# Main attention: the six prepared blocks of the next pair of heads placed at other score tiles

## The chip, the cores and the metric

The kernel runs on one core of one Trainium2 chip. The metric is the device time of one execution in microseconds (us). A core has TensorE (PE in the profile), VectorE (DVE), ScalarE (ACT), GpSimd (POOL) and SyncE (SP, which here issues the transfers). Each runs its own list of instructions in order, and they wait for each other on semaphores.

## The reference

Two transformer blocks on x of 1024 tokens by 256. The change lies in the first block's main attention, 16 heads over all 1024 tokens:

```
q_mid = rmsnorm(h @ q_a_w.T);  q = q_mid @ q_b_w.T          # per head: 128 nope + 64 rope
kv_lora, k_pe = split(h @ kv_a_w.T)                         # 64 latent, 16 heads x 64 rope
q_pe, k_pe = apply_rope(q_pe), apply_rope(k_pe)             # x * cos + rotate_half(x) * sin
scores = (q_nope.k_nope + q_pe.k_pe) * 192 ** -0.5
probs  = softmax(scores);  ctx = probs @ v;  main_out = ctx @ o_w.T
```

The key's nope part and the values come from the 64 latents, so the kernel folds those weights into the query: a head's score is a product over 64 rope rows and 64 latent rows. The rest (a 16-head pattern attention ahead of it, an 8-expert layer behind it, then the second block with a causal attention and 16 experts) is not touched.

## The kernel before

**Tiles and units.** The main attention works on pairs of heads p = 0 to 7. A pair has four units u = 4p to 4p + 3 (256 queries each), and a unit four score tiles (128 queries by 1024 keys of one head). `main_order` writes one list, and each engine takes from it the steps that are its own, in that order. A unit on PE is: six matmuls of score tile 0 (L1834 to L1836, `pe_score`), the output product of two units ago (L1972), tile 1, tile 2, half of the last unit's probabilities times values (128 small matmuls, L1938), tile 3, the other half. Scores are held in two slots of PSUM. DVE takes the maximum of a tile (L1843) and turns the exponentials (L1871), ACT takes the exponentials (L1858).

**Prepared blocks.** Before a pair's scores can start, its queries and keys have to be made from the latents, in six blocks of 128 x 512, in the order `FIRST = (R0, R1, R2, Q0, R3, Q1)`: R0 and R1 the rope keys (two halves of the tokens), R2 and R3 the rope queries, Q0 and Q1 the latent queries. A block k of pair p takes these steps:

- PE: five or six matmuls of 128 x 512 (`pe_prep`, L1569), after the copy of the block two before it.
- ACT: a copy out of PSUM into a staging tile t (`act_product`, L1623). There are two staging tiles, taken in turn, so a copy first waits until POOL and the transfers have let go of the block two before.
- SP, for rope blocks only: four transfers that swap rows inside t (`sp_swap`, L1637).
- POOL: for a rope block times cosine (L1650), then, with the swap landed, times sine (L1652), the sum (L1655), two roundings (L1669) and two remainders (L1676); for a latent block only the roundings and remainders. Behind Q0 it splits the next key weights, and behind Q1 the next latent and rope query weights (L1736 to L1758).

The first score tile of a pair waits for R0, R1, R2 and Q0 on POOL, the one of its third unit (4p + 2) for R3 and Q1. POOL's list has the blocks one behind the other and is not written by `main_order`.

**Places.** A block stands at a number of a score tile, counted from the first tile of the pair before it: number 4 is tile 0 of the second unit, 16 is tile 0 of the pair itself. Only numbers that leave 0 or 1 over when divided by 4 (tiles 0 and 1 of a unit) are asked for in `main_order`. On PE the block follows the output product or tile 1, on ACT it follows the exponentials of tile 0 (at tile 0) or stands ahead of those of tile 1 (at tile 1).

**SP's list.** Per unit SP has four transfers of the row sums (`sp_shares`, L1906) that wait for DVE's reciprocal (L1891 to L1898), two that spread them (`sp_spread`, L1919), and behind these the unit's swaps. At unit 28 it also issues the expert weights (L2302) once the last swap is out.

Of the kernel before, what the change touches and what calls it, by code (L numbers as in the profile page):

```python
# [71 lines left out]
    (31, 1): [("normed", 0)],  # L72
}

PREP_AT = (5, 8, 9, 12, 16, 17)


def main_order():

    order = [("expo", 0, 1), ("score", 0, 2), ("ctx", 0), ("ctx", 1), ("vturn", 0, 0), ("expo", 0, 2), ("score", 0, 3),  # L80
             ("cadd", 0), ("ctx", 2), ("vturn", 0, 1), ("cadd", 1), ("expo", 0, 3), ("ctx", 3), ("cadd", 2), ("vturn", 0, 2),
             ("cadd", 3)]
    preps = {16 * (p - 1) + at: (p, i) for p in range(1, 8) for i, at in enumerate(PREP_AT)}

    def prep(n, kind):
        if n in preps:
            order.append((kind, *preps[n]))

    def output(u):
        if u >= 0:  # L90
            order.extend([("project", u), ("add", u)])

    for u in range(1, 32):
        order.append(("score", u, 0))
        output(u - 2)
        prep(4 * u, "prep")
        order.extend([("rec", u - 1), ("spread", u - 1), ("vturn", u - 1, 3), ("expo", u, 0)])
        prep(4 * u, "pcopy")
        order.extend(BESIDE_LAST.get((u, 0), ()))
        order.append(("score", u, 1))  # L100
        prep(4 * u + 1, "prep")
        prep(4 * u + 1, "pcopy")
        order.extend([("vturn", u, 0), ("expo", u, 1)])
        order.extend(BESIDE_LAST.get((u, 1), ()))
        order.extend([("score", u, 2), ("pv", u - 1, 0), ("vturn", u, 1), ("expo", u, 2)])
        order.extend([("score", u, 3), ("pv", u - 1, 1), ("lift", u - 1), ("vturn", u, 2), ("ot", u - 1), ("expo", u, 3)])
    output(30)
    order.extend([("rec", 31), ("spread", 31), ("vturn", 31, 3), ("turn", 0), ("pv", 31, 0), ("pv", 31, 1), ("hT", 0),
                  ("wup", 1), ("wdown", 1), ("lift", 31), ("ot", 31), ("project", 31), ("logits", 0), ("add", 31)])
    return order  # L110
# [197 lines left out]
def program(nc, a, out):  # L308
# [841 lines left out]
    def act_fold(e, step):  # L1150
# [6 lines left out]
        else:  # L1157
            rows, dst, h0, _ = fold_rows(g - 4)
            e.activation(dst[0:rows, h0:h0 + 8, :].rearrange("p h c -> p (h c)"), bank[fold_bank(g)][0:rows, :],
                         ACT.Copy).then_inc(fold_ok, 1)  # L1160

    PATTERN, MAIN, CAUSAL = pattern_order(), main_order() + experts_order(), causal_order()

    g0, a0_ok, hf_ok, bias_ok, add_ok = (sem(n) for n in ("g0", "a0_ok", "hf_ok", "bias_ok", "add_ok"))
# [2131 lines left out]
```

## Time and profile before

| | |
|---|---|
| median of three runs | 1306.22 us (1299.85 to 1313.52) |
| the profiled execution | 1304.03 us, span 1302.2 us |
| busy in the span | PE 1189.6 us (91%), DVE 891.5 (68%), ACT 654.2 (50%), POOL 532.7 (41%) |
| main attention, from its first tile in this list to its last product | about 270 to 778 us of the span |
| chain that ended last | PE 61%, DVE 12%, POOL 12% |

A line of a timeline gives start, duration, engine, line and operation, and in brackets how long the engine had been idle before and for whom it waited. The matmuls overlap, so the distance from start to start tells more than a duration. The "granted clock" is 1.0 at TensorE's 2.4 GHz and 0.5 at 1.2 GHz.

### The profile page before, as it was taken

How to read it: one execution, taken by the hardware profiler on the slowest of the kernel's cores; microseconds unless marked ns; L12 is line 12 of the kernel's file. 1: busy time of each engine (PE TensorE's matmuls, PEld its weight loads, DVE VectorE, ACT ScalarE, POOL GpSimd, SP SyncE). 2: the span in 40 equal slices, each digit the busy share in tenths (PEclk: the TensorE clock that was granted, in tenths of full speed). 3: DMA queues.
4: the chain of work that ended last, by engine and by line, in shares of the span. 5: the costliest groups of instructions: out<-in, count | busy, mean ns of one | idle time of the engine just before them, and what ended most of it. 6: DMA issues, size and time to landing. Idle time of an engine off the chain costs nothing.

```text
span 1302.2 us, 34623 instructions
## 1 busy us (share of the span) xinstructions
PE 1189.6 (91%) x14433; PEld 836.3 (64%) x14436; DVE 891.5 (68%) x1354; ACT 654.2 (50%) x1242; POOL 532.7 (41%) x531
## 2 busy tenths in 40 slices
PE   8999999997979898979797869999998998989997
PEld 5544334466767676767675657888853444678997
DVE  4689988367868687868675875645668673755555
ACT  3479978853434343434342424333245676435553
POOL 4257264327576666657575323544200000421221
PEclk8989999999989898989898978999999999989999
DMA  7780000011111111101010122010332410101110
GB/s 276 206 178 2 2 17 25 1 45 32 31 30 32 31 40 27 45 25 44 23 35 21 58 63 85 25 52 23 85 73 64 94 37 1 34 17 33 50 41 33
DMA packets 41699, 66.25 MB, mean 51 GB/s; under 512 B 8476, under 2 KB 27676, under 8 KB 40604
## 3 DMA queue, kind: packets, MB, share of 16 engines
q1 hardware_dynamic: 41544, 64.04, 17.8%
q8 instruction: 115, 1.88, 0.6%
q14 instruction: 40, 0.33, 0.1%
HBM read 45.60 MB, written 8.45 MB: 42 GB/s over the span
## 4 chain that ended last, share of the span: by engine, by line
PE 61%; DVE 12%; POOL 12%; issue 4%; ACT 4%; SPq 3%; DMA 3%; POOLq 0%; ACTq 0%; DVEq 0%
PE bank L1478 8%; PE bank L2148 6%; PE bank L2149 6%; PE bank L2150 6%; PE bank L1435 4%; PE bank L1938 4%; POOL qk0l L1676 3%; PE bank L1834 3%; PE bank L1298 3%; PE bank L1569 2%; PE bank L1972 2%; PE bank L1836 2%; PE bank L1835 2%; PE bank L1415 2%; DVE mpc L1377 2%
## 5 line engine op out<-in xcount | busy, mean ns | idle before, releaser
L1843 DVE TENSOR_REDUCE nmq<-bank 128x1 f32<-128x1024 f32 x128 | 155.1, 1212 | 95.8 <-PE bank L1836 94.3
L1858 ACT ACTIVATE P<-bank,nmq 128x1024 f32<-128x1024 f32 x128 | 142.8, 1115 | 144.6 <-DVE nmq L1843 143.8
L1456 ACT ACTIVATE Pb<-bank 128x512 f32<-128x512 f32 (+3 forms) x355 | 180.7, 573 | 31.6 <-PE bank L1435 10.9
L1306 DVE TENSOR_REDUCE mp<-bank 128x2 f32<-128x1024 f32 x128 | 153.5, 1222 | 29.7 <-PE bank L1298 28.9
L1834 PE MATMUL bank<-qk1h,qk0h 128*128 128x512 f32 x256 | 113.3, 443 | 46.7 <-POOL qk0l L1676 39.8
L1871 DVE STREAM_TRANSPOSE PT<-P 128x1024 f32<-128x1024 f32 x124 | 151.8, 1224 | 0.9 <-ACT P L1858 0.9
L1938 PE MATMUL bank<-PT,kv 32*64 32x128 f32 x7936 | 137.0, 275 | 7.9 <-issue 7.8
L1938 PEld LDWEIGHTS bank<-PT,kv 32*64 32x64 f32 x7936 | 118.5, 130 | 34.0 <-issue 33.8
L1377 DVE TENSOR_REDUCE mpc<-bank 128x2 f32<-128x1024 f32 (+2 forms) x96 | 88.3, 953 | 44.4 <-PE bank L1365 22.0
L1478 PE MATMUL bank<-Pb,vx 128*17 128x256 f32 (+3 forms) x1222 | 107.1, 411 | 0.7 <-ACT OTa L1492 0.5
L1836 PE MATMUL bank<-qk1h,qk0l 128*128 128x512 f32 x256 | 104.4, 408 | 0.7 <-issue 0.7
L1835 PE MATMUL bank<-qk1l,qk0h 128*128 128x512 f32 x256 | 104.1, 406 | 0.7 <-issue 0.7
L1834 PEld LDWEIGHTS bank<-qk1h,qk0h 128*128 128x128 f32 x256 | 49.7, 194 | 66.8 <-issue 50.2
L1652 POOL TENSOR_TENSOR t<-t,sinT 128x512 f32<-128x512 f32 x32 | 41.0, 1281 | 99.7 <-DMA t<-t 99.7
L2123 POOL TENSOR_TENSOR cTt<-cTt,gab 128x256 f32<-128x256 f32 x8 | 6.1, 760 | 179.9 <-DVE cTt L2118 179.7
L2349 POOL TENSOR_TENSOR hl<-hf,hh 128x512 fp32r<-128x512 f32 x32 | 41.7, 1305 | 90.4 <-ACT hh L2336 90.4
L1949 ACT ACTIVATE other<-bank 64x256 f32<-64x256 f32 x64 | 24.3, 379 | 97.1 <-PE bank L1938 96.3
L1435 PE MATMUL bank<-qstr,kstr 64*128 64x512 f32 x256 | 71.5, 499 | 0.6 <-ACT Pb L1456 0.6
L2563 POOL TENSOR_TENSOR v1l<-wr,v1h 128x512 fp32r<-128x512 f32 x25 | 32.1, 1287 | 95.0 <-ACT v1h L2558 95.0
L1650 POOL TENSOR_TENSOR Rt<-t,cosT 128x512 f32<-128x512 f32 x32 | 41.1, 1284 | 68.6 <-ACT t L1623 65.7
L1435 PEld LDWEIGHTS bank<-qstr,kstr 64*128 64x128 f32 x256 | 28.3, 185 | 58.0 <-ACT Pb L1456 36.6
L1415 PE MATMUL bank<-qst,kst 107*128 107x512 bf16 (+3 forms) x192 | 53.9, 330 | 7.8 <-ACT qst L1402 3.5
(354 smaller groups left out, 2912.9 us busy)
## 6 DMA issues: line engine op xcount, KB each, us to landing
t<-t SPq DMA_DIRECT2D x128, 64.0 KB, 2.4
wr<-wf SPq DMA_DIRECT2D x25, 256.0 KB, 2.7
wraw<-wf SPq DMA_DIRECT2D x8, 768.0 KB, 4.4
scratch<-stgr SPq DMA_DIRECT2D x4, 1024.0 KB, 4.0
Rs<-shares SPq DMA_DIRECT2D x64, 64.0 KB, 2.8
scratch<-stg SPq DMA_DIRECT2D x8, 384.0 KB, 2.6
qst<-scratch SPq DMA_DIRECT2D x9, 256.0 KB, 7.6
owT<-owT SPq DMA_DIRECT2D x1, 2048.0 KB, 11.5
```

What stands on the lines that cost most here:

```text
L1306: e.tensor_reduce(mp[:, w % 3, :, j, kh], wide[slot][:], AX, ALU.max).then_inc(ring_ok, 1)
L1377: e.tensor_reduce(mpc[:, w // 2 % 3, a0:a0 + 2, j, kh], wide[slot][:, :, 0:c], AX, ALU.max).then_inc(ring_ok, 1)
L1435: e.matmul(bank[b][:], kst2[r, hp, kt * 128:kt * 128 + 128], qst2[r, hp, cols(half)], start=True, stop=True).then_inc(st_mm[0], 1)
L1456: e.activation(PBR[l][i % len(PBR[l])][:, 0:c], bank[b][:, 0:c], ACT.Exp, scale=0.25).then_inc(exp_ok[0], 1)
L1478: last = e.matmul(bank[6][32 * a:32 * a + 17, to:to + c], vx[:, t, h * 17:h * 17 + 17], PBR[l][i % len(PBR[l])][:, q0:q0 + c], start=(t == ...
L1834: e.matmul(o, qh[:, qs], kh[:, ks], start=True, stop=False)
L1835: e.matmul(o, qh[:, qs], kl[:, ks], start=False, stop=False)
L1836: last = e.matmul(o, ql[:, qs], kh[:, ks], start=False, stop=True)
L1843: e.tensor_reduce(nmq[:, n % 8:n % 8 + 1], scores(u, i), AX, ALU.max, negate=True).then_inc(mp_ok, 1)
L1858: e.activation(probabilities(u, i)[:], scores(u, i), ACT.Exp, bias=nmq[:, n % 8:n % 8 + 1], accum_out=sums[:, u % 2, i:i + 1]).then_inc(ex ...
L1871: e.transpose(PT[u % 2][:, :, c:c + 32], source).then_inc(pt_ok, 1)
L1938: last = e.matmul(rest[64 * c:64 * c + 64, g, 64 - 64 * c:192 - 64 * c], kv4[b % 4][rows, b // 4, :], transposed(u, b)[rows, :], start=(b ...
```

## The change

The six places of a pair's blocks become one tuple per pair. Pair 1 keeps its first four places and has R3 at 13 and Q1 at 16 (before: 16 and 17). Pairs 2 to 7 have R0 at 1, R1 at 5, R2 at 9, Q0 at 12, R3 at 13 and Q1 at 16 (before: 5, 8, 9, 12, 16, 17). What each block does is the same.

```diff
-PREP_AT = (5, 8, 9, 12, 16, 17)
+PREP_AT = ((5, 8, 9, 12, 13, 16),) + ((1, 5, 9, 12, 13, 16),) * 6
...
-    preps = {16 * (p - 1) + at: (p, i) for p in range(1, 8) for i, at in enumerate(PREP_AT)}
+    preps = {16 * (p - 1) + at: (p, i) for p in range(1, 8) for i, at in enumerate(PREP_AT[p - 1])}
```

In blocks per unit, the four units of a pair (from its own first unit) had 2 (its own R3 and Q1), 1 (next R0), 2 (R1, R2), 1 (Q0). Now they have 2 (own Q1, next R0), 1 (R1), 1 (R2), 2 (Q0, R3).

SP's list from the last unit of pair 0 (u = 3) through the first two of pair 1; L1637 is a swap, L1724 and L1730 are the loads of key and query weights. Before:

```order
L1724 DMA wks<-wkpe 128x256
L1906 DMA shares<-rrow 4x32 x4
L1919 DMA Rs<-shares 64x2x128 x2
L1906 DMA shares<-rrow 4x32 x4
L1919 DMA Rs<-shares 64x2x128 x2
L1637 DMA t_152<-t_152 32x512 x4
L1730 DMA wqs<-wqpe 128x256
L1906 DMA shares<-rrow 4x32 x4
L1919 DMA Rs<-shares 64x2x128 x2
L1637 DMA t_152<-t_152 32x512 x4
```

And now:

```order
L1724 DMA wks<-wkpe 128x256
L1906 DMA shares<-rrow 4x32 x4
L1919 DMA Rs<-shares 64x2x128 x2
L1637 DMA t_152<-t_152 32x512 x4
L1906 DMA shares<-rrow 4x32 x4
L1919 DMA Rs<-shares 64x2x128 x2
L1730 DMA wqs<-wqpe 128x256
L1637 DMA t_152<-t_152 32x512 x4
L1906 DMA shares<-rrow 4x32 x4
L1919 DMA Rs<-shares 64x2x128 x2
L1637 DMA t_153<-t_153 32x512 x4
```

The swap of pair 1's R3 went one unit ahead, and the swap of pair 2's R0 came into the first unit of pair 1, behind the load of the query weights.

ACT's list over the same place, from Q0's copy in u = 3 (L1623 is a block's copy, P the exponentials of a tile). Before:

```order
L1623 ACTIVATE t_153<-bank 128x512
L1858 ACTIVATE P_157,sums<-bank,nmq 128x1024
L1858 ACTIVATE P_158,sums<-bank,nmq 128x1024
L1949 ACTIVATE other<-bank 64x256 x2
L1858 ACTIVATE P_156,sums<-bank,nmq 128x1024
L1858 ACTIVATE P_157,sums<-bank,nmq 128x1024
L1623 ACTIVATE t_152<-bank 128x512
L1623 ACTIVATE t_153<-bank 128x512
L1858 ACTIVATE P_158,sums<-bank,nmq 128x1024
```

And now:

```order
L1623 ACTIVATE t_153<-bank 128x512
L1623 ACTIVATE t_152<-bank 128x512
L1858 ACTIVATE P_157,sums<-bank,nmq 128x1024
L1858 ACTIVATE P_158,sums<-bank,nmq 128x1024
L1949 ACTIVATE other<-bank 64x256 x2
L1858 ACTIVATE P_156,sums<-bank,nmq 128x1024
L1858 ACTIVATE P_157,sums<-bank,nmq 128x1024
L1623 ACTIVATE t_153<-bank 128x512
L1623 ACTIVATE t_152<-bank 128x512
L1858 ACTIVATE P_158,sums<-bank,nmq 128x1024
```

R3's copy moved up behind Q0's, and after the first tile of pair 1 come Q1's copy and then R0's of pair 2. POOL's list is row for row the same; on PE and ACT only the places of the blocks differ.

## Rows read from the trace of the kernel before

**Rows 1.** Waits of 270 to 760 us: total us, times, longest

```profile
POOL t L1652 <- DMA t<-t: 91.9, 20, 8.9
...
PE bank L1834 <- POOL qk0l L1676: 39.8, 7, 6.8
...
PE bank L1938 <- issue: 7.8, 11, 1.5
...
PE bank L1834 <- ACT P L1858: 5.6, 2, 4.0
```

**Rows 2.** Windows: six pairs, first tile of pair 1 to that of pair 7

```profile
core 0: us, PE busy (x) PEld busy (x) DVE busy (x) ACT busy (x) POOL busy (x), PEclk, DMA share, GB/s
...
325.10:698.40 373.30, 326.20 (x7008) 257.01 (x7008) 278.91 (x336) 153.99 (x276) 247.86 (x252) 0.94 0.12 32
```

**Rows 3.** Timeline of PE: start, us, line, count, idle before

```profile
325.11 0.47 PE L1834 MATMUL bank<-qk1h,qk0h 128*128 128x512 f32 x1 [3.85 <-POOL qk0l L1676]
...
431.53 1.13 PE L1972 MATMUL bank<-mo,OTm 128*128 128x256 f32 x4 [0.28 <-DVE OTm L1963]
...
448.26 0.77 PE L1834 MATMUL bank<-qk1h,qk0h 128*128 128x512 f32 x1 [6.07 <-POOL qk0l L1676]
...
450.96 1.53 PE L1972 MATMUL bank<-mo,OTm 128*128 128x256 f32 x4
452.14 0.59 PE L1569 MATMUL bank<-qah,wqh 128*128 128x512 f32 x1
...
463.15 0.50 PE L1834 MATMUL bank<-qk1h,qk0h 128*128 128x512 f32 x1
...
465.08 1.13 PE L1972 MATMUL bank<-mo,OTm 128*128 128x256 f32 x4 [0.28 <-DVE OTm L1963]
465.86 0.58 PE L1834 MATMUL bank<-qk1h,qk0h 128*128 128x512 f32 x1
...
477.95 1.13 PE L1972 MATMUL bank<-mo,OTm 128*128 128x256 f32 x4 [0.29 <-DVE OTm L1963]
```

**Rows 4.** Chain of waits, merged, one block's matmuls at the full clock

```profile
455.05 1.16 PE bank L1569 x5
```

**Rows 5.** Timeline of POOL, first and second unit of pair 3

```profile
462.80 1.28 POOL L1652 TENSOR_TENSOR t<-t,sinT 128x512 f32<-128x512 f32 x1 [7.07 <-DMA t<-t]
...
469.65 1.28 POOL L1669 CAST qk0h<-t 64x512 fp32r<-64x512 f32 x2
471.01 2.64 POOL L1676 TENSOR_TENSOR qk0l<-t,qk0h 64x512 fp32r<-64x512 f32 x2
...
476.27 1.29 POOL L1650 TENSOR_TENSOR Rt<-t,cosT 128x512 f32<-128x512 f32 x1
479.02 1.29 POOL L1652 TENSOR_TENSOR t<-t,sinT 128x512 f32<-128x512 f32 x1 [1.45 <-DMA t<-t]
...
483.17 2.64 POOL L1676 TENSOR_TENSOR qk1l<-Rt,qk1h 64x512 fp32r<-64x512 f32 x2
```

**Rows 6.** Timeline of SP, first unit of pair 3: the swap, the load behind

```profile
458.36 2.92 SPq L1637 DMA_DIRECT2D t<-t  x4
461.32 0.58 SPq L1730 DMA_DIRECT2D wqs<-wqpe  x1
```

**Rows 7.** Timeline of ACT, first unit of pair 3: the second copy

```profile
456.24 0.60 ACT L1623 ACTIVATE t<-bank 128x512 f32<-128x512 f32 x1 [1.94 <-PE bank L1569]
```

**Rows 8.** Groups of DVE's instructions, 270 to 760 us: busy, mean ns

```profile
L1894 DVE TENSOR_TENSOR rsum<-rsum,gat 128x4 f32<-128x4 f32 x31 | 14.0, 453 | 1.1
```

**Rows 9.** Timelines of SP, ACT, POOL and PE around unit 29

```profile
713.25 2.44 SPq L2302 DMA_DIRECT2D wraw<-wf  x2
...
726.58 0.63 ACT L2288 ACTIVATE wh<-wraw 128x512 fp32r<-128x512 f32 x1 [4.97 <-POOL wraw L2282]
...
725.28 1.27 POOL L2282 TENSOR_TENSOR wraw<-wraw,gab 128x512 f32<-128x512 f32 x1
...
728.36 0.73 PE L1834 MATMUL bank<-qk1h,qk0h 128*128 128x512 f32 x1 [3.97 <-ACT P L1858]
```

## The prediction

> **What bounds the kernel now.** I read the page first: PE is busy for 91% of the span, but the mean over the kernel says little of one stage, so I went to the waits of the main attention alone. There PE waits for another engine in one place that counts: the first score tile of a pair waits for the remainder that POOL writes last of Q0, 39.8 us in 7 waits [rows 1]. Its other waits are small: 5.6 us for exponentials, 7.8 us in 11 stops that end without a releaser in the profile (bare stops below). Then the windows of six pairs, from the first tile of pair 1 (325.1) to that of pair 7 (698.4): 373.3 us, in which POOL is busy for 247.9, 66%, and DVE for 278.9, 75% [rows 2]. So POOL is late without being full. What makes it late stands in the same list of waits: 91.9 us in which POOL waits for the swap of a rope block [rows 1].
>
> The timeline of pair 3 shows how. I measure from M, the start of a unit's output product on PE (L1972), since most steps hang on it. In the second unit of this pair M is 465.08 and in the third 477.95, which is 12.87 us for a unit with one block [rows 3]. In the second unit R0 of the next pair is made, and its times sine starts at 479.02, behind a wait for the swap, M + 13.94 [rows 5]. From there POOL needs 485.81 - 479.02 = 6.79 us to the end of the block, and a latent block takes 473.65 - 469.65 = 4.00 us [rows 5]. Before the change R1, R2 and Q0 come in the last two units, so R1's wait for its swap and then three blocks lie in a row ahead of the next pair's first tile. PE is through at 442.19 and starts at 448.26 [rows 3]. DVE and ACT are not in it: they sit idle in that gap too.
>
> **The change, term by term.** It adds and removes no instruction. POOL's list is the same.
>
> 1. Gaps of pairs 2 to 7. 39.8 less the 3.85 of pair 1 [rows 1, 3] is 35.9 us in six gaps. Do they close? The next pair's first tile now needs R2 (made in the third unit at tile 1, alone, just as R0 was in the second unit) and then Q0. With R0's measured distance, R2's sine starts at M2 + 13.94, where M2 is the third unit's product. R2 ends at + 20.73, Q0 about 4.05 later, and PE starts some 0.4 behind it (447.81 to 448.26 [rows 3]; the end is that of the same kind of block [rows 5]): M2 + 25.2. PE itself would be ready at 12.87 for the third unit, plus 10.66 (431.53 to 442.19, a last unit with one block [rows 3]), plus 1.16 for R3's five matmuls [rows 4]: M2 + 24.7. So 0.5 us per gap stays by these rows. If the swap lands 0.5 us sooner nothing stays; if DVE's small product L1894, which stands ahead of the swap's transfers on SP, waits longer, more does. It takes 0.453 us on average [rows 8]. I take 0.5 x 6 = 3.0 us, with 0 at one end and 2 us per gap, 12 us, at the other (four times the row's value). Term: 32.9 us.
>
> The Trainium skill (SBUF — State Buffer, "Who interferes with whom") says that a DVE instruction with two SBUF inputs and a GpSimd one that reads SBUF shut each other out for a whole instruction, and L1894 is such a one. POOL's instructions here take up to 1.29 us, and by that rule L1894 waits more often when POOL is busy for more of the time. Were each L1894 held by one full POOL instruction, 0.8 us more than its mean, the swaps would come that much later and about 5 us would be lost; the row's mean already holds what POOL does to it now, and I go by the row.
>
> 2. The slow clock behind a gap. Behind the 6.07 us of idling the granted clock is 0.5, 1.2 GHz. From the first tile to the product PE takes 450.96 - 448.26 = 2.70 us, against 465.08 - 463.15 = 1.93, and the product 452.14 - 450.96 = 1.18 against 465.86 - 465.08 = 0.78 [rows 3]. That is 1.2 us per gap, in six gaps 7.0 us. A wait of 0.5 us as above should not bring it: the waits of 0.28 us on the product leave the next matmuls fast [rows 3].
>
> 3. Pair 1. Its R0 to Q0 stay, so its first tile stays at 325.11, and the gap of 3.85 us ahead of it [rows 3] stays POOL's. But R3's 1.16 us on PE [rows 4] now lie inside this gap, and the last unit that had two blocks (u = 28) has one. Term: 1.2 us.
>
> 4. Unit 29. There ACT waits 4.97 us for POOL to scale expert weights (L2282 at 725.28, right behind Q1 of pair 7), and PE then waits 3.97 us for exponentials [rows 9]. In the new order R3 of pair 7 is copied a unit ahead, so POOL should be through with Q1 some 13 us after the pair's first tile (worked out in term 5), not 27 (725.28 against 698.4). SP's 3.1 us of the swap are gone ahead of the load of these weights at 713.25 [rows 9], so that load comes sooner too. I take the 3.97 us and 1.2 us of slow clock as in term 2: 5.2 us, between 0 (the load is then what is late) and 5.5.
>
> 5. Other waits, at no cost. R3 and Q1 are needed by the third unit, some 27 us behind the first product. From Q0's end POOL needs 1.2 us for the key weights, 1.4 for a cosine, 6.8 and 4.0: 13.4 us, which is M + 11 in the first unit. The copies on ACT: R0's copy of the next pair stands in the first unit at M + 5.3 (456.24 [rows 7]) and needs the staging tile of R3, whose swap by the same 13.94 lands at M3 + 13.9, which is about the next product (12.87 + 1.16 = 14.0 for a unit with two blocks). That leaves about 5 us. The key weights for R0 are split right behind Q0, 1.2 us, and asked for 5 us later. On SP R0's swap follows the query weights, 0.58 us, and is otherwise where R3's was, M + 7.4 [rows 6]; POOL is then busy with R3 and Q1 to M + 11 and with weights for 2.6 us more (473.65 to 476.27 [rows 5]), so the swap lands beside it. If this cover were gone R0 would come some 3 us later, with R1's swap due only 6 us behind R0's end. So it costs nothing.
>
> Sum: 32.9 + 7.0 + 1.2 + 5.2 = 46.3 us. The profiled execution took 1304.03 us, which gives 1257.7. The median of the runs, 1306.22, lies 2.2 us above it, so I forecast **1260 us** as the median. In its own range of terms (9 us less in term 1, 5 less in term 4; 3 and 0.3 more) it is 1256 to 1274. What is late next is PE itself: with the gaps shut a pair takes (373.3 - 32.9 - 7.0) / 6 = 55.6 us, and DVE's 278.9 / 6 = 46.5 us fit into that.
>
> **Rivals.**
>
> - *Bare stops come to light.* There are 11 stops of at most 1.5 us in 32 units [rows 1], and others may now be hidden in the gaps. One more full stop per pair is 7 x 1.5 = 10.5 us: 1270. For it: PE has never run two pairs without a pause in this stage. Against it: the units between the gaps run on end without one in most places. 0.12.
> - *Half the gap stays.* If R2's swap lands 3 us later than R0's did, because a swap now stands in SP's list in every unit, the gap is 3.5 us, as large as pair 1's, and about the full slow clock with it. Lost against the forecast: 6 x (3.0 + 1.2) = 25 us: 1285. For it: POOL waits 91.9 us for swaps, and the margin in term 1 is nil. Against it: SP's list around R2 in the third unit is that around R0 in the second now. 0.14.
> - *It does nothing.* If POOL's waits are only moved (each of the four swaps is waited for alone, as in the first unit at 7.07 us [rows 5]), the pair's pace stays POOL's: 247.9 us of work / 6 = 41.3 us and 4 x 5 us of waits make 61 us, and the time stays 1304 to 1306. Against it: the waits run beside the units' own 13 us each, which is the calculation of term 1. 0.07.
> - *Slower: ACT is held by a staging tile.* R0's copy stands ahead of the exponentials of the first unit's second tile, and everything of the softmax is queued behind it on ACT, so PE stops with the slots full. It decides from the point where R3's swap lands over 5 us later than reckoned in term 5, and each us beyond it is lost once a pair; unit 29 shows the price, 4.97 us on ACT for 3.97 on PE [rows 9]. To end slower it must eat the 46 us: a hold of 10 us costs 9 us of gap and 1.2 of clock, 61 us in six pairs, 1321. For it: R3 is now made in a unit with two blocks. Against it: 15 us of delay in a swap is far more than POOL's longest wait for one, 8.9 us [rows 1]. 0.05.
>
> **How the numbers follow.** The forecast has 0.62. The range 1248 to 1285 takes in its own range, the bare stops and half a gap; on the low side it leaves room for a faster run (the three runs spread by 7 us either way). About 2 in 10 lie outside. A measurement of this kernel tells about 1%, 13 us, from no change. Faster by over 1% (below 1293): forecast, stops and half gap, 0.88. Within 1%: 0.07. Slower by over 1%: 0.05.
>
> **What would show it.** In the waits of the changed kernel "L1834 <- POOL qk0l" should be one wait of 2 to 3 us and otherwise under 1 us each, 3 to 8 us in all; the granted clock of the six pairs should be 0.98 or more (0.94 [rows 2]); a pair should take about 55 us; POOL's wait for sine should stay, with R0 to R2 each starting it near M + 13 to 14. ACT's wait for L2282 should be under 1 us in unit 29. The prediction is wrong if PE waits for ACT or DVE where POOL was, if L1623 on ACT shows a wait for staging, or if the bare stops grow from 7.8 us to 15 or more.

## The result and the profile after

The changed kernel takes **1258.9 us** in the median of four runs (1256.83 to 1260.88), the kernel before 1309.87 us beside it (four runs, 1299.85 to 1314.93): a ratio of 0.962, with a 95% interval of 0.9554 to 0.9686. Its profiled execution took 1260.88 us, with a span of 1259.0 us, against 1304.03 and 1302.2 before. So the two traces differ by 43.2 us of span, and it is these that are split up here.

The waits of the main attention in the changed kernel, 270 to 740 us, as in [rows 1] (total us, times, longest):

```profile
POOL t L1652 <- DMA t<-t: 78.4, 17, 7.8
...
PE bank L1972 <- DVE OTm L1963: 16.2, 29, 5.0
...
PE bank L1938 <- issue: 12.3, 12, 1.7
...
PE bank L1834 <- POOL qk0l L1676: 4.0, 1, 4.0
...
ACT t L1623 <- POOL Rt L1650: 3.0, 1, 3.0
...
PE bank L1834 <- ACT P L1858: 2.9, 2, 1.6
```

PE's wait for POOL is 4.0 us in one place where it was 39.8 in seven [rows 1]. POOL still waits 78.4 us for swaps, but PE no longer pays for it in the six changed pairs, but for 0.2 us ahead of pair 7 (below). PE's largest wait is now the product's for DVE, 16.2 us. Of these, 8.6 stand ahead of the last two products, behind which no tile follows; before, it was 14.2 up to 790 us, 8.0 of them at the same two places. The bare stops have grown from 7.8 to 12.3 us.

The windows of the same six pairs, from the first tile of pair 1 to that of pair 7 (columns as in [rows 2]):

```profile
323.00:659.40 336.40, 320.47 (x7008) 251.28 (x7008) 276.49 (x334) 152.19 (x273) 248.40 (x253) 0.99 0.14 35
```

The 7008 matmuls of [rows 2] now take 336.4 us, 56.1 us a pair, where they took 373.3. The work of DVE, ACT and POOL is the same to within 3 us, and the granted clock is 0.99 instead of 0.94.

PE's timeline, changed kernel: pair 1's first tile; the product of pair 2's last unit, its last small matmuls, pair 3's first tile and the product behind it; and pair 7's first tile (start, us, line, count, idle before):

```profile
323.07 0.77 PE L1834 MATMUL bank<-qk1h,qk0h 128*128 128x512 f32 x1 [3.96 <-POOL qk0l L1676]
...
421.16 1.13 PE L1972 MATMUL bank<-mo,OTm 128*128 128x256 f32 x4 [0.28 <-DVE OTm L1963]
...
430.95 2.46 PE L1938 MATMUL bank<-PT,kv 32*64 32x128 f32 x128
...
433.33 0.50 PE L1834 MATMUL bank<-qk1h,qk0h 128*128 128x512 f32 x1
...
435.27 1.13 PE L1972 MATMUL bank<-mo,OTm 128*128 128x256 f32 x4 [0.28 <-DVE OTm L1963]
...
659.45 0.47 PE L1834 MATMUL bank<-qk1h,qk0h 128*128 128x512 f32 x1 [0.23 <-issue]
```

Pair 3's first tile, 6.07 us late at 448.26 before [rows 3], follows the last small matmul at 433.33 without any wait, and the product comes 1.94 us behind it (2.70 before), at the full clock. POOL's timeline of the same place:

```profile
421.98 1.29 POOL L1652 TENSOR_TENSOR t<-t,sinT 128x512 f32<-128x512 f32 x1 [6.36 <-DMA t<-t]
...
430.20 2.62 POOL L1676 TENSOR_TENSOR qk0l<-t,qk0h 64x512 fp32r<-64x512 f32 x2
```

M2 is the product at 408.61, so R2's times sine starts at M2 + 13.4 (13.94 reckoned), and Q0 ends at 432.82, 0.5 us ahead of the tile that needs it. That is not 0.5 us to spare: where a tile waited for POOL in the kernel before, it started 0.36 us behind Q0's end in six of the seven places and 0.45 in the seventh, so 0.36 us is what the hand-over takes.

**Where the 43.2 us went**, by the starts of the products (L1972):

| stretch | before | after | less | reckoned |
|---|---|---|---|---|
| start of the span to the product of u = 4 | 327.32 | 325.77 | 1.55 | 0 |
| u = 4 to u = 28 | 373.85 | 335.32 | 38.5 | 39.9 |
| u = 28 to the last product | 76.03 | 69.53 | 6.5 | 6.4 |
| the rest | 525.00 | 528.38 | -3.4 | 0 |

Here the product "of u = 4" is the one that PE makes in unit 4. Of the first line, 2.3 us are there at the product of u = 2 (292.80, now 290.46), ahead of nearly all that the change moves; they are no part of its effect. From there to u = 4 the changed kernel takes 0.8 us longer, where a second trace of it (after_again) takes 1.1 us less than before. The last line is no effect of the change either. There is a stretch of it, 135 matmuls in both kernels, that shows how such a difference can come about. Before, then after:

```profile
1126.50:1147.20 20.70, 20.62 (x135) 18.02 (x133) 17.73 (x60) 6.93 (x12) 7.98 (x10) 1.00 0.01 2
```

```profile
1081.60:1107.20 25.60, 25.52 (x135) 22.27 (x132) 17.68 (x60) 7.04 (x12) 7.93 (x10) 0.80 0.00 1
```

PE is busy to the last 0.1 us in both, and the granted clock is 1.00 in the one and 0.80 in the other: 4.9 us in a stage that nobody touched. The 0.80 is a mean of the two levels, as a window inside the second shows:

```profile
1083.20:1093.20 10.00, 10.00 (x38) 9.10 (x39) 4.31 (x18) 1.42 (x3) 1.64 (x3) 0.50 0.00 1
```

For these 10 us PE runs at 1.2 GHz, behind a wait of 0.72 us at 1081.18 that the kernel before has too, at 1126.11, without a slow stretch behind it. Over the whole rest the two traces have 29.2 and 26.6 us at 0.50, so the clock can account for about 1.3 of the 3.4 us; where the others went is not traced.

### The profile page after: what moved, and what is told of

Read it like the earlier page. It is cut to its first block, busy times and chain, and to the rows that moved or that the text cites. A ratio compares the mean times of both kernels' runs of the same rounds, so it can differ in the third digit from the quotient of the medians.

```text
span 1259.0 us, 34623 instructions
## 1 busy us (share of the span) xinstructions
PE 1177.3 (94%) x14433; PEld 825.6 (66%) x14436; DVE 890.4 (71%) x1354; ACT 654.0 (52%) x1242; POOL 532.2 (42%) x531
## 4 chain that ended last, share of the span: by engine, by line
PE 72%; DVE 14%; issue 4%; ACT 4%; POOL 3%; DMA 1%; SPq 1%; DVEq 0%; ACTq 0%; POOLq 0%
PE bank L1478 8%; PE bank L1938 7%; PE bank L2148 6%; PE bank L2149 6%; PE bank L2150 6%; PE bank L1569 5%; PE bank L1435 4%; PE bank L1834 4%; PE bank L1836 3%; PE bank L1835 3%; PE bank L1972 3%; PE bank L1298 3%; PE bank L1415 2%; DVE mpc L1377 2%; DVE nmq L1843 2%
## 5 line engine op out<-in xcount | busy, mean ns | idle before, releaser
L1306 DVE TENSOR_REDUCE mp<-bank 128x2 f32<-128x1024 f32 x128 | 153.5, 1222 | 27.3 <-PE bank L1298 26.6
L1938 PE MATMUL bank<-PT,kv 32*64 32x128 f32 x7936 | 137.2, 276 | 11.7 <-issue 11.0
L1938 PEld LDWEIGHTS bank<-PT,kv 32*64 32x64 f32 x7936 | 118.7, 131 | 37.9 <-issue 37.8
L1835 PE MATMUL bank<-qk1l,qk0h 128*128 128x512 f32 x256 | 101.3, 396 | 0.0
L1949 ACT ACTIVATE other<-bank 64x256 f32<-64x256 f32 x64 | 24.2, 379 | 101.1 <-PE bank L1938 100.3
L2148 PE MATMUL bank<-v1h,h1h 128*128 128x256 f32 x200 | 56.9, 285 | 2.5 <-POOL h1l L2607 1.5
```

Source lines behind the costliest of these rows:

```text
L1306: e.tensor_reduce(mp[:, w % 3, :, j, kh], wide[slot][:], AX, ALU.max).then_inc(ring_ok, 1)
L1835: e.matmul(o, qh[:, qs], kl[:, ks], start=False, stop=False)
L1938: last = e.matmul(rest[64 * c:64 * c + 64, g, 64 - 64 * c:192 - 64 * c], kv4[b % 4][rows, b // 4, :], transposed(u, b)[rows, :], start=(b ...
L2148: e.matmul(o, lh, rh, start=start, stop=False, **k)
```

## Experiments

"Gap" is the idle time of PE ahead of a pair's first tile, ended by POOL. The expectations call the prediction's own account Theory A. Its rival B has R3 and Q1 alone as the cause (the first tile of a pair waits because POOL is too busy), and C, in the two swap experiments, has POOL's own work as what sets the pace, whatever gaps are shut. Further letters are explained where they stand. S and L are two accounts of what sets PE's pace once the gaps are shut. The six places are those of `PREP_AT`. Medians are of four runs unless said, and ratios are against the kernel before on the same chip (its medians there: 1307.25 to 1308.87 us).

### One half of the change: late_pair_only

Only R3 and Q1 are moved, in all pairs; R0 to Q0 stay at 5, 8, 9 and 12. (Against the kernel before; the line of `preps` changes as in the change.)

```diff
-PREP_AT = (5, 8, 9, 12, 16, 17)
+PREP_AT = ((5, 8, 9, 12, 13, 16),) * 7
...
```

> Only R3 and Q1 moved (places 5, 8, 9, 12, 13, 16 for all pairs). Theory A (the gap ahead of a pair comes from R1, R2 and Q0 made in its last two units, and R1's place closes it): the first tile still comes 31 us behind the third unit's product, PE's gaps shrink only by R3's 1.2 us to about 4.8 each, unit 29's wait of ACT is gone. Saved 7 x 1.2 + 5.2 = 13.6 us: 1290, 5 or 6 gaps of 3 to 6 us left, clock 0.96. Rival B (what counts is that POOL loses its idle stretch at the start of a pair, where R3 is waited for): most of the gain is here, 1265 to 1270, gaps under 2 us.

Measured: 1289.38 us, ratio 0.9853 (0.9797 to 0.9909). The waits of this kernel, 270 to 760 us:

```profile
PE bank L1834 <- POOL qk0l L1676: 24.2, 7, 4.4
...
ACT t L1623 <- POOL Rt L1650: 19.4, 6, 3.6
```

All seven gaps are still there, 0.35 to 4.42 us each, so B is out: with R1, R2 and Q0 in a row the first tile stays late. Q0 ends no sooner behind the third unit's product than before (30.6 to 33.1 us, before 30.7 to 32.5); the gaps are shorter because PE gets there later. R3's five matmuls now lie in them, 1.16 us each, and PE stops elsewhere: R3's copy waits for its staging tile in six pairs, 19.4 us, which costs PE 4.0 us in four places, and the bare stops are 11.5 us.

### The other half: early_keys_only

R0 and R1 are moved ahead in pairs 2 to 7; R3 and Q1 stay at 16 and 17. (R0 is at 4 here and at 1 in the change.)

```diff
-PREP_AT = (5, 8, 9, 12, 16, 17)
+PREP_AT = ((5, 8, 9, 12, 16, 17),) + ((4, 5, 9, 12, 16, 17),) * 6
...
```

> Only the keys R0 and R1 of pairs 2 to 7 are moved one place, to 4 and 5 (R3 and Q1 stay at 16 and 17). Theory A: R1 is out of POOL's way before R2, but POOL is still behind with R3, Q1 and the weights until 11 us after the second unit's product, so R1 ends 13.6 us after the third unit's product, Q0 at 25.8, and PE, with only three blocks in the last three units, is ready at 23.5: gaps of about 2.8 us. Saved about 3.6 us a pair, 22 in all: 1283. Rival B: nothing but the shift of a block, under 5 us saved: 1300. Unit 29's wait of ACT stays 4 to 5 us either way.

Measured: 1291.62 us, ratio 0.9862 (0.9812 to 0.9911), some 9 us over the expectation. Its waits, 270 to 760 us:

```profile
ACT t L1623 <- POOL qk0l L1676: 33.5, 6, 7.0
...
PE bank L1938 <- ACT t L1623: 17.5, 6, 4.3
...
PE bank L1834 <- POOL qk0l L1676: 8.5, 5, 4.2
```

The gaps do nearly close, as Theory A has it: of the 8.5 us, 4.2 are pair 1's, which this edit leaves alone, and the four others are 0.7 to 1.4 us each. (In pair 6 the tile waits 2.1 us, put down to ACT, and it too starts 0.36 us behind Q0's end.) What is lost is lost elsewhere, and the timelines of ACT, POOL and PE show where:

```profile
411.61 0.60 ACT L1623 ACTIVATE t<-bank 128x512 f32<-128x512 f32 x1 [7.00 <-POOL qk0l L1676]
```

```profile
408.92 2.60 POOL L1676 TENSOR_TENSOR qk0l<-t,qk0h 64x512 fp32r<-64x512 f32 x2
```

```profile
412.46 3.27 PE L1938 MATMUL bank<-PT,kv 32*64 32x128 f32 x104 [4.33 <-ACT t L1623]
```

ACT waits 7.00 us to copy a block into a staging tile that POOL frees only with Q1's remainder, which ends at 411.52; the exponentials are queued behind the copy, and PE stops for 4.33 us. The held copy is R1's in all six pairs (4.9 to 7.0 us). That is the mechanism of the prediction's last rival, though there it was R0's copy held by R3. The two halves save some 19 and 17 us, and the whole 51: neither gives its full worth without the other. With R0 and R1 ahead, POOL must be rid of R3 and Q1 sooner, or ACT is held; with R3 and Q1 ahead alone, the first tile still stands behind three blocks. The halves do not add up to the change exactly, since R0's step from 4 to 1 is in neither.

### The swap ahead of the spread: before_swap_first and after_swap_first

In both kernels SP issues a unit's swaps behind the spread of the row sums, which waits for four transfers. Here SP keeps the spread back until the unit's score tile 2, so the swap goes out at once.

```diff
+        held = []
...
             elif s[0] == "spread":
-                sp_spread(e, s[1])
+                held.append(s[1])
+            elif s[0] == "score" and s[2] == 2 and held:
+                sp_spread(e, held.pop())
+        if held:
+            sp_spread(e, held.pop())
```

> The kernel before, with SP issuing a unit's swaps ahead of the spread of the row sums instead of behind it. Theory A (the swap's landing behind the row sums on SP is the first link of POOL's late chain): R1's swap lands 2.4 us sooner, PE's gaps of 4 to 6.8 us shrink by about as much, and so does that of pair 1: 7 x 2.4 = 17 us saved, 1290, POOL's wait for swaps falls from 92 to about 65 us. Rival C (POOL's own work of 41 us a pair sets the pace, and the waits only move): within 5 us of before, 1302 to 1309.

Measured: 1277.43 us, ratio 0.9759 (0.9715 to 0.9804): 31 us less than before, 13 us under the expectation. The gaps are down to 6.0 us in five, the longest 1.8, and short enough that the matmuls behind them stay fast: 1.46 to 1.47 us from tile to product, against 2.69 or 2.70 behind the gaps of 4.0 us and more in the kernel before. So in the kernel before SP's wait for the row sums is the first link of the chain that makes POOL late; I had the link right and its size too small. There is a price, in the waits of the same kernel:

```profile
PE bank L1972 <- DVE OTm L1963: 25.8, 25, 5.0
...
DVE OTm L1963 <- DMA Rs<-shares: 12.2, 9, 2.3
```

The product now waits for the late spread, 25.8 us where it was 14.2 up to the last product. The same edit on the changed kernel:

> The changed kernel with the same edit on SP's list. Theory A (in six pairs PE no longer waits for POOL): only pair 1 gains, its gap of 4.0 us becomes 1.6 and its slow clock goes: 1255 to 1257, against 1258.9. Rival C (POOL still sets the pace in the changed kernel, without a gap that shows): 10 us or more are saved, under 1250. In the other direction: if the spread of the row sums now lands too late, PE waits for OTm, over 1265.

Measured: 1261.43 us, ratio 0.9639 (0.9586 to 0.9691). No gain is to be seen over the changed kernel's 0.962. The gap of pair 1 falls from 3.96 to 0.49 us, and the product's wait rises from 16.2 to 26.6 us. With the blocks spread out the swaps are soon enough (Q0 now ends 4.4 to 6.3 us ahead of the tile in the six pairs), and what is left of the edit is its price. Rival C is out.

### How near the edge: after_late_swap

Each swap of pairs 2 to 7 is cut into eight transfers of half the columns instead of four, so it lands later.

```diff
-            swapped_[z_] += 64
+            swapped_[z_] += 128 if p_ > 1 else 64
...
-        for q in range(4):
-            e.dma_start(t[32 * (q ^ 1):32 * (q ^ 1) + 32, 1, :], t[32 * q:32 * q + 32, 0, :]).then_inc(SWAPS[p, k][0], 16)
+        for q, cs in itertools.product(range(4), (cols(0),) if p < 2 else (slice(0, 256), slice(256, 512))):
+            e.dma_start(t[32 * (q ^ 1):32 * (q ^ 1) + 32, 1, cs], t[32 * q:32 * q + 32, 0, cs]).then_inc(SWAPS[p, k][0], 16)
```

> The changed kernel, with each swap of pairs 2 to 7 cut into eight transfers of half the columns instead of four. Issue takes about 0.6 us each, so the last one leaves some 2.4 us later and the same bytes land. Theory A (R2's swap is the first link, and it has 0.3 to 4.9 us to spare, 0.3 to 0.5 in three pairs): POOL's Q0 comes 2.4 us later, gaps of about 2 us in three pairs, 0.5 in the others: 7 to 12 us lost with some slow clock, 1267. Rival D (SP's row sums stand behind the longer swaps and PE waits for OTm): waits of L1972 grow, over 1275. Rival E (there is slack of more than 2.4 us everywhere): within 3 us of 1258.9.

Measured: 1264.98 us, ratio 0.967 (0.9645 to 0.9696), near the 1267 of Theory A; the interval overlaps the changed kernel's, so the time alone does not decide, but the gaps do. The first tiles of this kernel on PE that wait for POOL:

```profile
326.05 0.52 PE L1834 MATMUL bank<-qk1h,qk0h 128*128 128x512 f32 x1 [3.98 <-POOL qk0l L1676]
...
384.59 0.77 PE L1834 MATMUL bank<-qk1h,qk0h 128*128 128x512 f32 x1 [2.52 <-POOL qk0l L1676]
...
441.33 0.47 PE L1834 MATMUL bank<-qk1h,qk0h 128*128 128x512 f32 x1 [1.82 <-POOL qk0l L1676]
```

R2's times sine starts 2.1 to 2.9 us later behind its product than in the changed kernel. Of the six gaps four come back, 5.7 us in all (behind the two shown, 0.40 and 1.00), and a fifth, 2.17 us in pair 7, is put down to ACT's exponentials but also starts 0.36 us behind Q0's end. In the changed kernel Q0 ends 0.36 to 4.9 us ahead of the tile; less the 0.36 of the hand-over that leaves nothing in pairs 2 and 7, 0.15 us in pair 3, and 1.7 to 4.5 us in pairs 4 to 6. The margin of term 1 is as thin as the prediction had it.

### More of the same: after_pair1, after_pair1_again and after_all_early

Pair 1 is the one whose first four blocks the change leaves alone. In after_pair1 its R0 and R1 come ahead too:

```diff
-PREP_AT = ((5, 8, 9, 12, 13, 16),) + ((1, 5, 9, 12, 13, 16),) * 6
+PREP_AT = ((4, 5, 9, 12, 13, 16),) + ((1, 5, 9, 12, 13, 16),) * 6
```

> The changed kernel with pair 1 at 4, 5, 9, 12, 13, 16, so R0 and R1 in its first possible unit. Theory A: pair 1 had its gap of 4.0 us because R1, R2, Q0 lay in its last two units as before the change; now R2's swap comes alone and the gap closes: 4.0 us and 1.2 of slow clock saved, 1253.7. Rival F (pair 1 is late because POOL is late from the stage ahead): no gain, 1258 to 1260, since the gap of 4 us stays.

Measured: 1252.67 us, ratio 0.9579 (0.9555 to 0.9604). The gap of pair 1 is gone; the longest wait for POOL at a first tile is now 0.38 us. It was run again beside the changed kernel itself, six runs of each:

> The changed kernel with pair 1 at 4, 5, 9, 12, 13, 16 once more, beside the changed kernel on the same chip: 4 to 6 us below it (the gap of 4.0 us and its slow clock), 0.957 to 0.959 of before.

> The changed kernel as it is, on the chip of this call, as the reference for the run beside it and for the one with pair 1 moved: 1256 to 1262, ratio to before 0.962. Where the bare stops of PE stand at fixed places of its list, they stand after the same counts of matmuls as in its first profile (2464, 3479, 5375, 6261, 8286, 9173, 10187); if they come from what happens beside PE at that moment, they are elsewhere.

Measured: 1252.01 us, ratio 0.9548 (0.9513 to 0.9583), against 1255.16, ratio 0.959 (0.9559 to 0.962). Both times the median is lower, by 6 (against another chip's runs) and by 3 us (expected 4 to 6), and the intervals overlap, so the gain is not shown by the times. It has the lowest median of the versions that compute everything, and probably rightly so, since a wait of 3.96 us is gone.

In after_all_early R2 and Q0 come ahead as well, which gives POOL more time ahead of every pair:

```diff
-PREP_AT = ((5, 8, 9, 12, 13, 16),) + ((1, 5, 9, 12, 13, 16),) * 6
+PREP_AT = ((4, 5, 8, 9, 13, 16),) + ((1, 4, 8, 9, 13, 16),) * 6
```

> Places 4, 5, 8, 9, 13, 16 for pair 1 and 1, 4, 8, 9, 13, 16 for the rest: Q0 is made three places sooner, so POOL has over 5 us to spare ahead of each pair. Theory A (PE is the bound in these pairs, and the 0.3 to 0.5 us to spare were enough): the same as with pair 1 alone moved, 1252 to 1255. Rival C: if the thin margin still cost something, 5 us less again, under 1250. If two blocks in a unit cost PE more than the blocks themselves, 1258 or more.

Measured: 1257.65 us (six runs), ratio 0.9636 (0.9603 to 0.9669). There are no gaps, and no gain either; the time is above Theory A's 1252 to 1255 and near the 1258 of the third account, by which two blocks in a unit cost PE more than the blocks themselves. What the traces show is that slack ahead of a tile that is not late is worth nothing. In pair 1 the four early blocks bring the rival's hold: ACT waits 5.79 us for a staging tile at 302.92, and PE's small matmuls 3.33 us for ACT.

### What PE is held by once the gaps are shut: after_less_pe and after_less_small

after_less_pe leaves out one of the three products of a score tile in pairs 1 to 7 (L1835), a third of the matmuls of these tiles; the numbers of the lines behind it are one higher.

```diff
-            e.matmul(o, qh[:, qs], kl[:, ks], start=False, stop=False)
+            if p == 0:
+                e.matmul(o, qh[:, qs], kl[:, ks], start=False, stop=False)
```

> The changed kernel without the product of the query's high part with the key's low part in the scores of pairs 1 to 7 (two of a tile's six matmuls; the scores are less exact): 2 x 0.23 us less on PE per tile, 7.4 us a pair. Theory A (PE is the bound now, and POOL's chain is only 0.3 to 0.5 us behind it): the first two units of a pair shorten by 3.7 us, but the first tile then waits for POOL as before, gaps of 3 to 4 us with slow clock come back in most pairs; saved about 6 x 2.5 + 7 for the last pair = 22 us: 1237. Rival G (POOL has room): the whole 7 x 7.4 = 52 us are saved, 1207. Rival C (POOL is already the bound): nothing saved but the last pair's 7 us, 1252.

Measured: 1255.07 us, ratio 0.9599 (0.9569 to 0.963), where 1237 was expected. No gap came back in the six pairs: Q0 ends 2.8 to 5.1 us ahead of the tile. Its windows of the six pairs, and its waits in them:

```profile
322.90:652.90 330.00, 283.97 (x6816) 217.99 (x6816) 276.65 (x334) 152.60 (x272) 249.73 (x254) 0.99 0.14 36
```

```profile
PE bank L1939 <- issue: 24.2, 23, 1.9
PE bank L1973 <- DVE OTm L1964: 16.4, 22, 0.8
PE bank L1834 <- POOL qk0l L1676: 4.0, 1, 4.0
```

192 matmuls that started 0.23 us apart are gone, 44 us (36.5 of PE's busy time), and the six pairs are only 6.4 us shorter. What grew in their place is above all the bare stops, from 8.4 us in nine at L1938 (changed kernel, same six pairs) to 24.2 in 23, and then the product's waits, from 6.2 to 16.4: 26 of the 37.6 us that are missing. The rest stays open.

after_less_small takes away number instead of time: half of the small matmuls (L1938) of units 4 to 31, those of half the keys.

```diff
         for b in range(16 * part, 16 * part + 16):
+            if u >= 4 and b % 4 // 2 != part:
+                continue
```

> The changed kernel without half of the small matmuls of probabilities times values in units 4 to 31 (64 instead of 128 in each of the two parts of a unit; half of the keys are left out). It cuts about the time on PE that the run with four matmuls a tile cut, 2.0 us a unit against 1.85, but 256 of PE's some 580 instructions of a unit (a matmul counts with its weight load), against 16. In that run only 6.4 of 44 us in six pairs were saved, and PE's bare stops grew from 8.4 to 24.2 us. Theory S (PE is held by how fast its list comes in, at about 24 ns an instruction in both, 336.4 / 14016 and 330.0 / 13632): the stops vanish, the six pairs fall from 336 us to 295 to 305, where PE's work and DVE's 46 us a pair meet: 1215. Theory L (the softmax loop over DVE and ACT holds a unit at 13.7 us whatever PE does): as little as in that run, 325 to 332 us, 1250, and few stops, with waits for OTm and P instead.

Measured: 1220.31 us, ratio 0.9312 (0.9279 to 0.9344), near S's 1215 and far from L's 1250. Its windows of the six pairs:

```profile
322.19:619.67 297.48, 272.54 (x4064) 207.87 (x4065) 276.52 (x335) 153.31 (x275) 248.38 (x253) 0.99 0.15 38
```

38.9 us are saved, with PE's busy time down by 47.9. There is no bare stop in these pairs (one of 0.9 us in all of 270 to 760), and the gaps come back: 13.8 us in seven, 4.4 of them pair 1's and 1.1 to 2.0 each in the other six. POOL is again what is late.

Counted by instructions the three fit together. The changed kernel has 14,016 matmuls and weight loads in the six pairs, 24.0 ns each; after_less_pe has 13,632, 24.2 ns each; after_less_small 8,129, 36.6 ns each. The first two have the same pace per instruction, though PE is busy for 36.5 us less in the second. Only where the list is much shorter does the work itself, or POOL, set the time.

The bare stops lie at fixed places of that list. The windows from the start of the span to the same two stops, first of the changed kernel, then of after_again, then of the kernel before (PE's count of matmuls is the number behind its busy time):

```profile
1.00:299.76 298.76, 288.52 (x2463) 147.68 (x2464) 219.15 (x297) 211.22 (x430) 135.10 (x148) 0.99 0.30 83
...
1.00:673.70 672.70, 639.80 (x10187) 422.49 (x10187) 522.44 (x663) 377.95 (x729) 412.49 (x428) 0.99 0.22 58
```

```profile
1.00:299.53 298.53, 286.89 (x2463) 146.42 (x2464) 218.63 (x297) 211.34 (x430) 135.15 (x148) 0.99 0.30 83
...
1.00:666.10 665.10, 635.30 (x10187) 419.07 (x10187) 520.83 (x663) 378.50 (x729) 412.70 (x428) 0.99 0.21 58
```

```profile
1.00:302.15 301.15, 291.35 (x2463) 148.12 (x2464) 218.81 (x297) 211.48 (x430) 135.17 (x148) 0.98 0.30 82
...
1.00:716.00 715.00, 651.07 (x10187) 431.05 (x10187) 523.60 (x663) 378.32 (x729) 404.52 (x420) 0.96 0.20 53
```

The time of the stop differs by up to 50 us, the work beside PE differs, and the stop comes before the same matmul. The stops of the changed kernel in this stage stand at 2464, 3479, 5375, 5502, 6261, 6390, 7276, 7528, 8286, 9173 and so on, always a multiple of about 126.6 matmuls apart. Not every place of this grid has a stop in every run: of the 13 of the changed kernel behind 280 us, nine are in after_again, which has five others. Counted in all instructions of PE's list, with the loads and the waits on semaphores, the grid is one of 256 instructions: in the six pairs of the changed kernel, after_again, after_less_pe and the kernel before every bare stop stands on it, within one. The one exception is the 0.23 us ahead of pair 7's first tile, which starts 0.36 us behind Q0's end and so is a wait for POOL.

The Trainium skill (Runtime: NRT & Kernel Launch, "Instruction fetch mechanics") says that an engine's instructions are fetched in blocks of 256 and that the cost of crossing into the next is mostly hidden. The distance agrees; "hidden" does not, with 12.3 us of stops in 470 us and 24.2 in 330. The traces hold the transfers too, on a queue of their own. Its rows on the pages of the changed kernel, after_less_pe and after_less_small (packets, MB, share):

```profile
q8 instruction: 115, 1.88, 0.6%
```

```profile
q8 instruction: 113, 1.85, 0.6%
```

```profile
q8 instruction: 87, 1.43, 0.5%
```

PE's list has 29,472, 29,027 and 22,307 instructions in these traces, 115, 113 and 87 blocks of 256, so this queue brings PE's list, a packet a block. The trace has the time of each packet. Every bare stop of the six pairs ends 1.2 to 1.6 us after a packet landed: ten in the changed kernel, ten before, 25 in after_less_pe. A block's first matmul comes within 2 us of a landing at 29 of 55 places in the changed kernel, at 35 of 54 in after_less_pe, and at 5 of 32 in after_less_small, where none is a stop. So PE stands at a bare stop until its next block is there, and what S says holds for these stops. What makes a packet come so late is not traced, and no run changes the fetching alone.

## Why the prediction was right, step by step

1. **Gaps of pairs 2 to 7 (32.9 reckoned).** All but 0.2 of the 35.9 us went; the 3.0 that were to stay did not. R2's sine starts at M2 + 13.2, 13.4, 12.0, 12.9, 12.3 and 13.5 in the six pairs, up to 2 us sooner than R0's 13.94 from which I reckoned. That was one unit's value: in the trace of before R0's are 13.06, 14.18, 13.93, 13.88, 13.10 and 12.41, and their mean, 13.4, leaves no gap. Q0 ends at M2 + 22.8 to 24.3, and the tile starts at M2 + 24.4 to 24.7 in pairs 2, 3 and 7, as reckoned for PE (24.7). In pairs 4 to 6 it starts at 26.2 to 28.1, because PE is later itself, by its bare stops in part; most of the slack there is PE's lateness and not POOL's earliness. POOL's chain as the cause stands: half of the change leaves seven gaps (late_pair_only), an earlier swap alone all but shuts them (before_swap_first), a later one opens most of them again (after_late_swap). What the term did not see is that the new order needs both halves: with R0 and R1 ahead alone the gaps nearly close, but ACT is held instead. The 5 us that one full POOL instruction per L1894 would have cost did not come: it takes 456 ns in the mean, 453 before [rows 8], with POOL busy for 74% of the time instead of 66%. The hold itself is plain in the trace, though. The changed kernel's DVE and POOL at a free L1894 and at a held one:

```profile
370.01 0.16 DVE L1894 TENSOR_TENSOR rsum<-rsum,gat 128x4 f32<-128x4 f32 x1
...
437.25 0.90 DVE L1894 TENSOR_TENSOR rsum<-rsum,gat 128x4 f32<-128x4 f32 x1
```

```profile
436.84 1.29 POOL L1655 TENSOR_TENSOR Rt<-Rt,t 128x512 f32<-128x512 f32 x1
```

   The held one ends at 438.15, 0.02 us behind POOL's instruction. Of the 32 L1894, 16 take 0.17 us or less before the change and 12 now; all others end 16 to 27 ns behind the end of a POOL instruction and take up to 1.18 us. The Trainium skill's rule (SBUF — State Buffer, "Who interferes with whom") thus agrees with the trace, and as the prediction said of it, more of them are held when POOL is busier: 20 instead of 16. But a hold lasts only for what is left of POOL's instruction, and the sum of all went from 9.0 to 9.4 us.
2. **Slow clock (7.0).** Right behind the gaps: the clock of the six pairs is 0.99, and tile to product takes 1.94 to 1.97 us in pairs 3 to 6. But the bare stop of 1.66 us at 583.38 has a slow stretch behind it, at 0.50 from 584.8 to 588.0: the three large matmuls and 128 small ones that fall in it take about 1.5 us more than elsewhere.
3. **Pair 1 (1.2).** R3's matmuls were to lie inside the gap, which should then show 2 to 3 us; it is 3.96, so PE came no later to it. The trace of before has a bare stop of 1.47 us in this stretch (316.32) that the new one has not. u = 28 has one block less. R3's copy in pair 1 waits 3.03 us for POOL, which holds nobody up. The gain shows in u = 28, 17.18 to 14.95 us from product to product, which is 2.2 us where 1.2 were reckoned.
4. **Unit 29 (5.2).** The stretch behind it, from 718.35 to 735.45 before, is 4.2 us shorter. Together with term 3: 6.5 us against 6.4. ACT's wait for L2282 is gone from this unit, but PE still waits 1.26 us for exponentials at the tile where it waited 3.97:

```profile
683.36 0.50 PE L1834 MATMUL bank<-qk1h,qk0h 128*128 128x512 f32 x1 [1.26 <-ACT P L1858]
```

   The changed kernel's POOL and ACT there:

```profile
675.32 1.28 POOL L2282 TENSOR_TENSOR wraw<-wraw,gab 128x512 f32<-128x512 f32 x1 [4.08 <-issue]
```

```profile
678.26 1.05 ACT L2268 ACTIVATE wh<-wraw 128x1024 fp32r<-128x1024 f32 x1
679.21 0.62 ACT L2288 ACTIVATE wh<-wraw 128x512 fp32r<-128x512 f32 x1
```

   POOL is through with the scaling at 676.6, 2.6 us ahead of ACT, which before waited 4.97 us for it [rows 9].
5. **Other waits (0).** ACT, POOL and DVE cost PE nothing that a row shows, as said. There is one wait for a staging tile, the 3.0 us in pair 1; the prediction had named such a wait as a sign of being wrong, and it stops PE nowhere. But "what is late next is PE itself", with its work, was only half of it. The bare stops between the products of u = 4 and u = 28 went from 6.3 to 9.7 us, which is 3.4 us (0.2 of it the wait ahead of pair 7): the gaps gave 35.9 and the clock 7.0, 42.9 in all, less 3.4 is 39.5, and the stretch gave 38.5. The last 1.0 is no more than what the slow stretch of item 2 takes, about 1.5. A caution on sizes: after_again, the same kernel, takes 331.6 us for this stretch instead of 335.3, with 7.5 us of bare stops instead of 9.7, so terms of 1 to 3 us are as large as what two traces of one kernel differ by. after_less_pe shows that more of them would come if PE had less to do.

The sum was 46.3 and the span gave 43.2: 3.0 more in term 1, 3.4 less for the stops, 1.55 more ahead of u = 4, 3.4 less behind the stage, and 1.0 less that the slow stretch can account for. The mechanism is shown, but that the sum is off by no more than 3.1 us is luck in part, with errors of 3.0 to 3.4 us in it both ways. The median, 1258.9, lies 1.1 us under the forecast of 1260, and 51 us under the 1309.87 measured beside it, where the forecast had 46.

Of the rivals, the bare stops came true in part, with 4.5 us more of them where 10.5 had been priced. Half a gap did not stay; but in three of the six pairs Q0's end lay no more than 0.5 us ahead of the tile, which is the hand-over and next to nothing more. That nothing happens was ruled out by term 1's own calculation. The hold of ACT by a staging tile did not come here, but it is no remote case: early_keys_only has it in six pairs, and its table differs only in R3 and Q1 at 16 and 17 instead of 13 and 16, and R0 at 4 instead of 1.

## What to carry to other kernels

When an engine with time to spare is late for one tile, measure its steps from a common event of the program (here the product of the unit before), in the unit where the step stands alone, and add them up in the new order; here it told that six gaps close to within 0.5 us each. Take the mean of all units that you have for such a distance, not one. Look at what frees the buffers that the moved steps fill: a move that is right by the needs of the tile can put its wait on the engine that fills the buffer, and two moves may be worth more together than the sum of both: here 19 and 17 us alone, and 51 together. And when the last gap is shut, count the instructions of the busiest engine beside its busy time, since less work in nearly as many instructions may give little (here 6.4 us for 44).

## What the runs showed of the hardware that was not expected

- PE's bare stops, 0.2 to 2.2 us each, stand on a grid of 256 instructions of its list, and those of the six pairs end 1.2 to 1.6 us after a 16 KiB packet on the queue "q8 instruction" has landed. Six pairs of the changed kernel take 24.0 ns per instruction and of after_less_pe 24.2, though 128 small matmuls and their 128 loads go through in 2.1 us.
- A DVE product of 0.16 us with two inputs in SBUF took up to 1.18 us, ending 16 to 27 ns behind the end of an instruction of POOL: 16 of 32 times before, 20 of 32 in the changed kernel.
- 44 us of large matmuls less gave 6.4 us; 48 us of busy time less in 5,887 fewer instructions gave 38.9.
- A stretch of 135 matmuls that no edit touched took 20.70 us at a granted clock of 1.00 in one run and 25.60 in another, where the clock was 0.50 for 10 us of it, with PE busy throughout in both.
- An order of transfers that puts a swap some 2 to 3 us sooner saved 31 us in one kernel and nothing in the next.
